# Third attention: values of two pairs of heads projected at once, in passes of 256 columns in place of 128

## The reference, cut to what matters

```python
q = (query @ w_q).reshape(B, Q, 16, 64).transpose(0, 2, 1, 3)
k = (key @ w_k).reshape(B, Kl, 16, 64).transpose(0, 2, 1, 3)
v = (value @ w_v).reshape(B, Kl, 16, 64).transpose(0, 2, 1, 3)
scores = jnp.einsum('bhqd,bhkd->bhqk', q, k) * scale
attn = jax.nn.softmax(scores, axis=-1)
out = jnp.einsum('bhqk,bhkd->bhqd', attn, v)
out = out.transpose(0, 2, 1, 3).reshape(B, Q, 16 * 64)
return out @ w_o
```

## Time and profile before

| | |
|---|---|
| median of 3 runs | 2137.42 us (2136.59 to 2137.57) |
| the profiled execution's own time | 2139.27 us |
| its span, from first to last instruction | 2137.5 us |
| mean granted TensorE clock over the span | 0.937 |
| TensorE busy | 1916.8 us, 90% |
| VectorE busy | 1300.3 us, 61% |
| ScalarE busy | 1295.9 us, 61% |
| third attention, first to last scores | 795.1 to 1603.5 us of the span |

### The profile page before, as it was taken

How to read it: one execution, slowest core, us unless ns; L and a number is a source line. 1 busy time by engine, 2 the same in 40 slices (tenths; PEclk the granted TensorE clock), 3 DMA queues, 4 the chain that set the end, 5 groups by cost and what they waited for, 6 DMA issues and landing times. The chain is left out here.

```text
span 2137.5 us, 43664 instructions
## 1 busy us (share of the span) xinstructions
PE 1916.8 (90%) x17168; PEld 1358.0 (64%) x17168; DVE 1300.3 (61%) x3193; ACT 1295.9 (61%) x2088; POOL 134.0 (6%) x347
## 2 busy tenths in 40 slices
PE   6999999966868559999999999999994699999997
PEld 4677777734734537777777777777772456666664
DVE  6888888876445335545555545555555776666663
ACT  4999999954348116555555555555553456666664
POOL 4000000000022110000000000000000400000000
PEclk9999999976969679999999999999996789999999
DMA  6211111102070520000000000000000621111110
GB/s 232 57 46 42 47 43 46 42 16 75 9 182 2 154 77 1 1 2 1 1 2 1 2 1 1 2 1 2 1 2 12 197 61 47 42 47 41 47 41 17
DMA packets 55292, 87.71 MB, mean 41 GB/s; under 512 B 9866, under 2 KB 31422, under 8 KB 55090
## 3 DMA queue, kind: packets, MB, share of 16 engines
q1 hardware_dynamic: 54577, 83.87, 13.3%
q0 software_dynamic: 512, 1.05, 0.2%
HBM read 66.93 MB, written 17.96 MB: 40 GB/s over the span
## 5 line engine op out<-in xcount | busy, mean ns | idle before, releaser
L2402 ACT ACTIVATE a_prT<-bank 128x512 f32<-128x512 f32 (+1 forms) x448 | 232.7, 565 | 328.3 <-PE bank L2311 328.1
L1173 DVE CUSTOM_DVE_ANT_0 a_attn_junk<-wide,a_mask 128x801 f32<-128x801 f32 (+1 forms) x256 | 247.5, 991 | 122.0 <-PE wide L1003 121.8
L1114 ACT ACTIVATE a_attn_prT<-bank 128x512 f32<-128x512 f32 (+1 forms) x448 | 237.0, 566 | 121.8 <-PE bank L1020 109.6
L2429 DVE CUSTOM_DVE_ANT_0 a_sc<-wide,a_zeros 128x1024 f32<-128x1024 f32 (+1 forms) x256 | 243.1, 987 | 91.5 <-PE wide L2297 91.5
L1470 DVE CUSTOM_DVE_ANT_0 a_attn_sc<-wide,a_mask 128x801 f32<-128x801 f32 (+1 forms) x256 | 252.9, 989 | 11.9 <-PE wide L1319 10.2
L1335 PE MATMUL bank<-ident,a_attn_sc 128*128 128x128 f32 x1664 | 244.4, 275 | 15.3 <-ACT a_attn_prT L1427 14.1
L1335 PEld LDWEIGHTS bank<-ident,a_attn_sc 128*128 128x128 f32 x1664 | 198.8, 142 | 62.3 <-issue 42.3
L2311 PE MATMUL bank<-ident,a_sc 128*128 128x128 f32 x1664 | 231.3, 277 | 1.5 <-ACT a_prT L2402 1.5
L2311 PEld LDWEIGHTS bank<-ident,a_sc 128*128 128x128 f32 x1664 | 185.1, 141 | 54.4 <-issue 28.1
L2363 PEld LDWEIGHTS bank<-a_prT,a_vt 128*64 128x64 f32 x3328 | 180.3, 137 | 48.4 <-issue 47.0
L2297 PE MATMUL wide<-a_kT,a_qT 64*128 64x512 f32 (+1 forms) x1024 | 211.0, 529 | 0.0
(11 more groups left out here) (443 smaller groups left out, 2542.7 us busy)
## 6 DMA issues: line engine op xcount, KB each, us to landing
a_ks<-a_k_parts SPq DMA_DIRECT2D x384, 75.0 KB
a_k_parts<-a_proj_kp SPq DMA_DIRECT2D x24, 416.0 KB, 4.5
a_qx<-a_q_stack SPq DMA_DIRECT2D x384, 12.0 KB
moe_w1b<-in_e_w SPq DMA_DIRECT2D x15, 256.0 KB, 2.9
ctxT<-in_ctxT SPq DMA_DIRECT2D x4, 832.0 KB, 10.7
a_ctxn<-in_ctxn SPq DMA_DIRECT2D x4, 832.0 KB, 12.2
m_q_stack<-m_proj_qp SPq DMA_DIRECT2D x9, 256.0 KB
m_ks<-m_k_parts SPq DMA_DIRECT2D x24, 96.0 KB
```

Source lines behind the costliest of these rows:

```text
L1114: act.activation(prT[0:keys, u % PRT, kt:kt + m, :], bank_of(s, f"W{g}")[0:keys, 0:m * S].rearrange("p (t q) -> p t q", q=S), ACT.Exp).the ...
L1173: dve.tensor_tensor_reduce(junk[:, n % 2, 0:w], S_WIDE[n % 2][:, 0:w], mask(qt, at, w), 1.0, LOWEST, ALU.add, ALU.max, mx[:, p % 2, qt, e, ...
L2402: copy = lambda out, src: act.activation(out, src, ACT.Copy)
L2429: dve.tensor_tensor_reduce(sc[:, s % 2, h, at:at + w], S_WIDE[h][:, 0:w], zeros[:, 0:w], 1.0, LOWEST, ALU.add, ALU.max, mx[:, s % 2, h, p: ...
```

## The change

The values of two groups (two pairs of heads of one batch, whose weight columns lie side by side) are projected together. A matmul has 256 columns, two of them fill a slot, and 13 serve two groups. They lie in two V steps: in steps with s % 4 = 3 four slots with two context tiles each (tiles 0 to 7), in steps with s % 4 = 1 slots with 2, 2 and 1 tiles (8 to 12) and no X3. The value buffer `vt` holds two such double groups. `values` waits, once in four steps, for the last copy of the step before it. The wait counts (`made`, `by_act`, `by_dve`) follow from `has`.

```diff
     def has(s, k):
         kind = SLOTS[k][0]
+        if kind == "X" and s % 2 == 1:
+            return value_blocks(s, int(SLOTS[k][1:])) is not None
         return 1 <= s <= STEPS if kind == "T" else 2 <= s <= STEPS + 1 if kind == "O" else (s + 2) // 2 < GROUPS
+
+    def value_blocks(s, i):
+
+        j, first = ((s + 1) // 4, 2 * i) if s % 4 == 3 else ((s - 1) // 4, 8 + 2 * i)
+        return (j, first, min(2, KT - first)) if 2 * j < GROUPS and first < KT else None
...
-        vt = core.sb(ctx, name + "_vt", [P, 2, KT, P], F32)
+        vt = core.sb(ctx, name + "_vt", [P, 2, KT, 2 * P], F32)
...
                 else:
-                    for kt in range(4 * i, min(4 * i + 4, KT)):
-                        ins = pe.matmul(bank[:, (kt % 4) * P:(kt % 4 + 1) * P], core.ctxT[:, b, kt * P:(kt + 1) * P],
-                                        wv[:, cols], start=True, stop=True)
+                    j, first, m = value_blocks(s, i)
+                    b, p, _, _ = place(4 * j)
+                    for n in range(m):
+                        ins = pe.matmul(bank[:, 2 * P * n:2 * P * (n + 1)], core.ctxT[:, b, (first + n) * P:(first + n + 1) * P],
+                                        wv[:, p * P:(p + 2) * P], start=True, stop=True)
...
             def values(s):
                 t = s - 2
-                _, _, slot, _ = place(t)
                 pe.wait_ge(freed_by_act, by_act[s - 1, 10])
-                if t % 2 == 0:
-                    pe.wait_ge(freed_by_dve, by_dve[s - 3, 11])
+                if t % 4 == 0:
+                    pe.wait_ge(freed_by_dve, by_dve[s - 1, 11])
...
-                        ins = pe.matmul(U_BANK[DH * h:DH * (h + 1), 0:P], vt[:, slot, kt, DH * h:DH * (h + 1)],
+                        at = t // 2 % 2 * P + DH * h
+                        ins = pe.matmul(U_BANK[DH * h:DH * (h + 1), 0:P], vt[:, t // 4 % 2, kt, at:at + DH],
...
-                _, _, slot, _ = place(s + 2)
-                m = min(4, KT - 4 * i)
-                copy(vt[:, slot, 4 * i:4 * i + m, :], bank[:, 0:m * P].rearrange("p (t q) -> p t q", q=P)).then_inc(freed, 1)
+                j, first, m = value_blocks(s, i)
+                copy(vt[:, j % 2, first:first + m, :],
+                     bank[:, 0:2 * m * P].rearrange("p (t q) -> p t q", q=2 * P)).then_inc(freed, 1)
```

## The result

The changed kernel takes 2143.46 us (median of 18 runs, 2139.58 to 2149.05) against 2139.05 us before (18 runs, 2136.57 to 2142.38). The ratio is 1.0027, 95% interval 1.0020 to 1.0033. The forecast was 2142.8 / 2137.42 = 1.0025, so the time lies inside the range and the direction holds. With more runs the median of before rose from 2137.42, that of its first 3 runs, to 2139.05. The two medians of 18 runs lie 4.4 us apart (0.21%), the ratio gives 5.8 us with an interval of 4.3 to 7.1.

The account below looks back on a forecast made before the run. TensorE was taken to bound the kernel, with VectorE's drain 0.23 us from holding it in V steps. 15 x 0.37 - 0.1 = +5.4 us on 2137.42 gave 2142.8 us, range 2140.9 to 2144.7.

Parts of the forecast that it names:

- The price of a pass: TensorE's value matmuls: a 256-column pass in a stream takes 217.5 ns, by a straight line between 111 and 430 ns.
- the lower bound of 215: A 256-column pass at half of the 512-column pass's 430 ns; the whole sum would then be +4.5 us.
- Rival (c): Value matmuls: wide pass cheaper than the line, 14 ns for no change, 25 for a gain; chances 0.02 and 0.02.
- The long step: V steps with s % 4 = 3: X3 grows by 0.65 us uncovered, X0 to X2 save 0.06, so +0.59 us.
- The short step: V steps with s % 4 = 1: 0.04 us saved ahead of O, 0.18 of 0.675 behind it usable, so -0.22 us.
- The wait: Short step's end: next scores held by VectorE's drain of head 1, so 0.49 of 0.675 us freed becomes waiting.
- The usable slack: Between VectorE's drain of head 1 and the values in short steps: 0.18 us of the 0.675 freed behind O.
- The overlap of the two heads: Scores after short steps: time from head 1's weights to the values stays 1.92 us despite head 0's early start.
- rival (b): Scores after short steps: staggered heads run one after the other, +23 us, or +6.5 in a small form; chance 0.07.
- The first pair: Prologue (s = -1) and step 1: +0.61 us in the prologue, -0.72 in step 1, together -0.1 us.
- What would show it: Profile after: steps of 13.02, 11.97, 13.5, 13.27 us; score weight loads naming VectorE some 15 times at about 0.45.
- The sum: Whole kernel: 15 pairs of V steps at +0.37 us, less 0.1 for the first pair, make +5.4 us.

Follow-up runs that it names:

- X2 doubled: Changed kernel with one 256-column value matmul of slot X2 done twice in each short step after s = 1; four steps 51.73 us, ratio to before 1.0026.
- X2 tripled: Changed kernel with one 256-column value matmul of slot X2 done three times in each short step after s = 1; four steps 52.10 us, ratio to before 1.0044.
- X3 doubled: Changed kernel with one value matmul of slot X3 done twice in each long step, prologue excepted; four steps 52.17 us, ratio to before 1.0060.
- the control: Kernel before, unaltered, timed against itself; four steps 51.41 us, ratio 1.0009 (0.9997 to 1.0021).
- the two versions with lighter slots ahead of O: Changed kernel with short-step slots 1, 1, 2, 1 (split 8 and 5) or 2, 1, 2, 1 (split 7 and 6); ratios to before 0.9982 and 0.9987.

## Where the prediction was right and where it failed, step by step

**In short.** The mechanism was right: the long step pays, the short step's freed time becomes VectorE's wait of 0.50 us, and the heads keep their overlap. The step that failed is a term of the sum, the price of the wide pass: forecast 217.5 ns, measured 215.9. With it a pair of V steps was costed at +0.37 us where it costs +0.32, 0.7 us too much in 15 pairs. The time came out as near as 2142.8 to 2143.46 by luck in part: against that excess stands a base of three runs whose median (2137.42) lay 1.6 us under that of 18 runs.

**The price of a pass** was forecast at 217.5 ns by a straight line between 128 and 512 columns. Measured by the starts in a stream in the trace after it is 215.9 ns, between the line and the lower bound of 215, for which the prediction's sum was +4.5. Rival (c) needed a pass 14 ns under the line for no change at all; it lies 1.6 under it. The line took one fixed part for all widths. By the earlier trace rows a column costs (430 - 111) / 384 = 0.83 ns, which at the granted clock of 1.00 (2.4 GHz) is two clocks. The estimate from the Trainium skill's fixed cost, 220 ns, was further off, because it took the 2.5 ns away from two value passes of 111 ns, which carry more than that. Over two clocks a column the wide pass lies 2.6 ns (213.3), the transposes of 128 columns at 109.2 ns lie 2.5 (106.7), the narrow value passes at 111.6 ns 4.9, and the passes of 512 columns, 431.5 ns from start to start, 4.8 (426.7). The fixed cost of the page, "TensorE: Matmul & The Clock Gate", section "Wait — 56ns, not 53.3ns?", agrees with the first two, if it is taken over these two clocks a column, and not with the others. What the narrow value passes pay above it, 2.4 ns, was saved as well; that their longer weight load (0.19 us against 0.14) is the cause is argued, not shown.

**The long step** was forecast at +0.59 and measured at +0.56 (13.247 against 12.686, medians of the stage). **The short step** with what it does to the step behind it was forecast at -0.22: measured (11.945 + 13.521) - (12.683 + 13.024) = -0.24. Together +0.32 in place of +0.37, nearly all of it the size of the pass: 24 passes that count x 1.6 ns = 0.04.

**The wait** was forecast at 0.49 us, measured at 0.50. The usable slack was forecast at 0.18, from one case at the stage's end; from the drain's end to the values it is now 1226.22 - 1224.24 = 1.98 us, where the earlier trace rows have 1225.66 - 1223.51 = 2.15: 0.17. **The overlap of the two heads** held, so rival (b) falls: 1.91 us from head 1's weights to the values in every short step's wake. **The first pair:** step 1 gave back 0.68 us (9.577 to 8.902), where 0.72 was forecast. In the prologue the time from the first projection to the first scores rose from 12.30 us to 12.52 and 13.16 in the two traces, where 0.61 was forecast. What differs between the executions is the granted clock, which rises from 0.50 to 1.00 within the prologue. Five traces have this prologue (the changed kernel twice, X2 doubled, X2 tripled, X3 doubled). The rise comes 6.2, 6.5, 6.7, 7.5 and 7.9 us behind their first projection, and the prologue takes 12.52, 12.68, 12.77, 13.16 and 13.24 us. In both traces of before the rise comes at 7.0 and the prologue takes 12.30 and 12.32. Between the neighbours of 7.0 it would be about 12.9 with the change, an estimate from these times: +0.6, as forecast, for an equal clock.

**What would show it.** Forecast steps 13.02, 11.97, 13.5, 13.27, measured 13.02, 11.95, 13.52, 13.25. These held, the next sign did not. The scores' weight loads were forecast to name VectorE about 15 times at 0.45 us; the list of what ended the idle time ahead of the scores' instructions (us in total, times) says this for the changed kernel:

```profile
  ACT a_prT L2411: 7.5, 30
  DVE a_mx L2438: 4.7, 19
```

And this for the kernel before:

```profile
  DVE a_mx L2429: 1.6, 4
```

19 - 4 = 15 times is right, but (4.7 - 1.6) / 15 = 0.2 us each, not 0.45: the loads' idle time begins only when head 0's two are through (1223.80 + 0.29 = 1224.09 in the timeline above, to 1224.31), so the view shows less than half of the wait. So this sign of the prediction was wrong in size: it took the whole wait for idle time of the loads. The 30 for ScalarE are gaps of 0.17 and 0.33 us at the change to the scores, ahead of head 0's loads in 15 steps each, with a late releaser; before, this view counted the gaps at these places as issue, time in which nothing that the profile shows was waited for.

**The sum.** 15 x 0.32 - 0.68 + 0.2 to 0.9 in the prologue is 4.3 to 5.0 us, against 5.4 forecast; with the prologue at an equal clock it is 4.7. From the first key projection to the last scores the traces have 820.7 us in both executions of before and 824.7 and 825.3 after, +4.0 and +4.6 (before includes 0.35 us in one step, see below). The medians of 18 runs give 4.4 us, the ratio 5.8 with an interval of 4.3 to 7.1. The difference of about 1 us between the traces' sum and the ratio is no larger than what the control shows for a kernel against itself, and stays open at that size.

## What to carry to other kernels

When a bound engine's work is moved between steps, count the step that gets more in full, and for the step that gets less ask which other engine it then waits for: the slack there (0.23 us here, 0.18 of it usable), not the freed time (0.68), is the gain. Work taken away ahead of the instruction that starts the other engine's chain is gained in full here, work taken away behind it only up to the slack, so an uneven remainder belongs ahead of it. An engine at 100% in every window can still wait when its instructions run in pairs; look at the distance of the pair's starts.

## What the runs showed beyond that

Two heads' fp32 passes do not wait for each other in the order of the program. In the trace of before at the end of step 62 passes start at 1594.54, 1595.08, 1595.51 and 1595.94 us, and at 1595.16, 1595.70, 1596.13 and 1596.56; by their distances the first four are head 0's, the others head 1's, which is inferred, since the rows don't name the head. So head 0's third pass starts before head 1's second, while in an ordinary step the heads' passes start in pairs 7 ns apart. Neither order delays the head that comes last.

The prologue differs between executions: TensorE's granted clock is 0.50 there, the lower of its two levels (1.2 GHz), and then rises to full (2.4 GHz), in the two traces of the changed kernel at about 787.5 us of the span, in the others between 785.8 and 790.1. The later it rises behind the first projection, the longer the projections ahead of the first scores take. The window from 787 to 790 us in the first trace of the changed kernel:

```profile
787.00:790.00 3.00, 2.35 (x9) 1.33 (x8) 1.21 (x3) 0.00 (x0) 0.00 (x0) 0.92 0.00 0
```

The same window in its second trace:

```profile
787.00:790.00 3.00, 1.93 (x6) 0.82 (x5) 0.88 (x3) 0.39 (x1) 0.00 (x0) 0.90 0.00 0
```

In the first the projections began at 781.30 us, in the second at 780.08, with the rise at nearly the same time, so the second did more of them at the lower clock: 13.16 us in place of 12.52.

Step 46, a K step like any other in the program, takes 13.38 us in place of 13.02 in both traces of the kernel before, and so it does in the two versions with lighter slots ahead of O; in the other seven traces no step of the stage's middle deviates. The window of step 46 before:

```profile
1377.98:1391.36 13.38, 13.14 (x109) 8.71 (x108) 6.84 (x17) 7.79 (x14) 0.00 (x0) 1.00 0.01 2
```

TensorE is idle in it for 0.24 us, where its neighbours have no idle time. VectorE is idle for 1.17 us ahead of the first add behind O in it, where it is 0.82 in step 33, and TensorE then waits for the second add. What held VectorE the trace does not show.
